# Cross attention in fp32r on one core: the stationary operands moved to other remainders by 512 bytes

## What is computed

```python
x_q = jnp.einsum('oc,bcn->bno', w_qk, y)
x_k = jnp.einsum('oc,bcn->bon', w_qk, x)
x_v = jnp.einsum('oc,bcn->bon', w_v, x) + b_v[None, :, None]
energy = jnp.einsum('bnc,bcm->bnm', x_q, x_k)
attention = jax.nn.softmax(energy, axis=-1)
attention = attention / (1e-07 + attention.sum(axis=1, keepdims=True))
x_r = jnp.einsum('bcn,bnm->bcm', x_v, attention)
x_r = jax.nn.relu(jnp.einsum('oc,bcn->bon', w_t, x - x_r) + b_t[None, :, None])
return x + x_r
```

## Time and profile before

| | us |
|---|---|
| median of 3 runs | 1866.73 |
| lowest, highest | 1864.39, 1866.74 |
| the profiled execution, its own time | 1866.61 |
| its span, first to last instruction | 1864.7 |
| TensorE matmul busy in the span | 1856.5 |
| VectorE, ScalarE, GpSimd busy | 1503.8, 1307.4, 780.7 |
| mean granted TensorE clock | 0.999 |

### The profile page before, as it was taken

One profiled execution on the slowest core, in us unless ns is written; L12 is line 12 of the kernel. 1 busy time (PEld: TensorE's weight loads), 2 busy tenths in 40 slices (PEclk: granted clock), 3 DMA queues, 4 the chain that ended last, 5 costly groups with the idle time before them and its releaser, 6 DMA issues.

```text
span 1864.7 us, 26374 instructions
## 1 busy us (share of the span) xinstructions
PE 1856.5 (100%) x8884; PEld 1565.2 (84%) x8884; DVE 1503.8 (81%) x2036; ACT 1307.4 (70%) x1793; POOL 780.7 (42%) x415
## 2 busy tenths in 40 slices
PE   9999999999999999999999999999999999999999
PEld 7888888888888888888888888888888888888887
DVE  6888787887877878878778788787787877877877
ACT  6677766677666776667766677766677666776664
POOL 4542444533444334444244452444533444424430
PEclk9999999999999999999999999999999999999999
DMA  3011211111110111101111111111011110111100
GB/s 107 30 62 46 69 67 51 39 45 68 67 68 23 64 49 67 68 23 67 45 67 68 39 51 45 67 68 62 28 52 61 68 67 23 68 45 68 68 9 37
DMA packets 33946, 101.92 MB, mean 55 GB/s; under 512 B 4208, under 2 KB 4976, under 8 KB 33904
## 3 DMA queue, kind: packets, MB, share of 16 engines
q1 hardware_dynamic: 33360, 101.46, 15.6%
q10 hardware_dynamic: 544, 0.00, 0.0%
HBM read 67.90 MB, written 33.55 MB: 54 GB/s over the span
## 4 chain that ended last, share of the span: by engine, by line
PE 97%; DVE 2%; ACT 1%; issue 0%; DVEq 0%
PE pv L693 36%; PE row_b L601 19%; PE row_a L601 14%; PE pv L669 9%; PE row_a L661 5%; PE row_b L661 5%; PE row_a L652 4%; PE row_b L652 4%; DVE colsum L445 0%; DVE p_lo L452 0%; PE pv L766 0%; DVE p_sb L427 0%; PE pv L661 0%; DVE gx_lo L387 0%; PE pv L770 0%
## 5 line engine op out<-in xcount | busy, mean ns | idle before, releaser
L201 POOL TENSOR_TENSOR y_lo<-y_raw,y_hi 128x896 fp32r<-128x896 f32 x128 | 279.1, 2203 | 566.2 <-ACT y_hi L258 377.1
L452 DVE SCALAR_TENSOR_TENSOR p_lo<-p_sb,row_inv,p_hi 128x1024 fp32r<-128x1024 f32 x256 | 328.9, 1286 | 98.3 <-ACT p_hi L304 98.3
L287 ACT ACTIVATE ev<-row_b 128x512 f32<-128x512 f32 x384 | 229.4, 597 | 202.9 <-PE row_b L601 202.9
L186 POOL TENSOR_TENSOR x_lo<-x_sb,x_hi 128x1024 fp32r<-128x1024 f32 x63 | 152.6, 2423 | 446.8 <-ACT x_hi L246 446.8
L304 ACT ACTIVATE p_hi<-p_sb,row_inv 128x1024 fp32r<-128x1024 f32 x256 | 292.4, 1142 | 32.8 <-PE pv L693 30.7
L296 ACT ACTIVATE p_sb<-p_sb,neg_max 128x1024 f32<-128x1024 f32 x256 | 295.1, 1154 | 25.5 <-DVE neg_max L427 21.5
L445 DVE SCALAR_TENSOR_TENSOR colsum<-p_sb,row_inv,colsum 128x1024 f32<-128x1024 f32 x224 | 289.6, 1293 | 8.5 <-DVE row_inv L435 0.6
L427 DVE CUSTOM_DVE_ANT_0 p_sb<-row_a,ev 128x1024 f32<-128x1024 f32 x128 | 156.5, 1223 | 146.7 <-PE row_a L601 141.8
L693 PE MATMUL pv<-p_lo,z_hi 128*128 128x512 f32 x1024 | 273.9, 389 | 0.5 <-DVE p_lo L452 0.5
L693 PE MATMUL pv<-p_hi,z_hi 128*128 128x512 f32 x1024 | 273.7, 389 | 0.0
L693 PE MATMUL pv<-p_hi,z_lo 128*128 128x512 f32 x1024 | 273.7, 389 | 0.0
(11 more groups left out here) (128 smaller groups left out, 3594.6 us busy)
## 6 DMA issues: line engine op xcount, KB each, us to landing
x_sb<-x SPq DMA_DIRECT2D x64, 512.0 KB, 4.8
out<-res SPq DMA_DIRECT2D x62, 512.0 KB, 2.9
y_raw<-y SPq DMA_DIRECT2D x64, 256.0 KB, 3.7
y_raw<-y SPq DMA_DIRECT2D x32, 512.0 KB, 3.7
out<-res SPq DMA_DIRECT2D x4, 256.0 KB, 2.0
res<-w_qk SPq DMA_DIRECT2D x1, 256.0 KB, 3.6
res<-w_t_T SPq DMA_DIRECT2D x1, 256.0 KB, 7.4
res<-w_v SPq DMA_DIRECT2D x1, 256.0 KB, 7.4
```

What stands on the lines that cost most here:

```text
L186: nc.gpsimd.tensor_tensor(x_lo[par][:, kt, :], x_sb[par][:, kt, :], x_hi[par][:, kt, :].bitcast(FP32), ALU.subtract).then_inc(x_lo_done, 1)
L201: nc.gpsimd.tensor_tensor(y_lo[:, :, cols], y_raw[:, 1:8, cols], y_hi[:, :, cols].bitcast(FP32), ALU.subtract).then_inc(y_lo_done, 1)
L287: nc.scalar.activation(ev[:, to, :], bank_b, ACT.Copy, scale=scale).then_inc(b_copied, 1)
L452: nc.vector.scalar_tensor_tensor(out=p_lo[r][:, :], in0=p_sb[r][:, :], scalar=row_inv[:, j:j + 1], in1=p_hi[r][:, :].bitcast(FP32), op0=AL ...
```

## The change

The stationary tensors g, z, wtT and y, and the moving tensor hnT, are allocated behind `res`, each pair with a gap tensor ahead that nothing reads or writes. No instruction is changed.

```diff
-        g_hi, g_lo = sb("g_hi", [P, KT, C], FP32R), sb("g_lo", [P, KT, C], FP32R)
-        hnT_hi, hnT_lo = sb("hnT_hi", [P, KT, C], FP32R), sb("hnT_lo", [P, KT, C], FP32R)
-        wtT_hi, wtT_lo = sb("wtT_hi", [P, KT, C], FP32R), sb("wtT_lo", [P, KT, C], FP32R)
...
-        y_hi, y_lo = sb("y_hi", [P, 7, BANK], FP32R), sb("y_lo", [P, 7, BANK], FP32R)
...
-        z_hi, z_lo = sb("z_hi", [P, NT, C], FP32R), sb("z_lo", [P, NT, C], FP32R)
...
         res = sb("res", [P, KT, N])
 
+
+        sb("gap_g", [P, 32])
+        g_hi, g_lo = sb("g_hi", [P, KT, C], FP32R), sb("g_lo", [P, KT, C], FP32R)
+        sb("gap_z", [P, 32])
+        z_hi, z_lo = sb("z_hi", [P, NT, C], FP32R), sb("z_lo", [P, NT, C], FP32R)
+        sb("gap_wtT", [P, 16])
+        wtT_hi, wtT_lo = sb("wtT_hi", [P, KT, C], FP32R), sb("wtT_lo", [P, KT, C], FP32R)
+        sb("gap_y", [P, 16])
+        y_hi, y_lo = sb("y_hi", [P, 7, BANK], FP32R), sb("y_lo", [P, 7, BANK], FP32R)
+        sb("gap_hnT", [P, 16])
+        hnT_hi, hnT_lo = sb("hnT_hi", [P, KT, C], FP32R), sb("hnT_lo", [P, KT, C], FP32R)
```

## The result

| | before | after |
|---|---|---|
| median, us | 1865.56 | 1889.80 |
| lowest, highest | 1864.05, 1866.74 | 1888.33, 1890.00 |
| profiled execution, its own time | 1866.61 | 1890.00 |
| its span | 1864.7 | 1888.1 |

The ratio is 1.0125, with a 95% interval of 1.0113 to 1.0137: the change makes the kernel slower, by 24 us. I had forecast no change.

What follows compares the result with a forecast made beforehand. TensorE was taken to bound the kernel, by matmul count times start spacing. Five family terms and the gaps, 0 each, left the forecast at 1866.6 us, beside a median of 1866.73; the range was 1815 to 1912.

Steps and rivals of the forecast that it cites:

- What bounds the kernel: TensorE, busy 1856.5 of 1864.7 us: time is the number of matmuls times the distance between their starts.
- The value I take: 0: Start-to-start spacing of the matmuls on TensorE: the new addresses change it by 0 ns; no change had chance 0.42.
- five families: Matmuls p on z, gx on y, x on wtT, x on g, hnT on x: spacing change forecast as 0 each.
- three rows: Trace evidence for 0: a matmul without weight load, equal 226.7 ns in L693 and L652, L661 unmoved by other SBUF users.
- The lone matmul: Matmul starting at 33.02 us, no weight load beside it: lasts 0.39 us like its neighbours, so loads cost it nothing.
- The second and third rows: L693 and L652 share no tensor or address yet have 226.7 ns; L661 keeps 119.6 ns while DMA, VectorE, GpSimd work.
- Rival A: Shifted addresses act like the late load, 5.0 ns per 512-column matmul: +36 us, 1903, or 1910 with L661; chance 0.30.
- late weight load: Load at 601.18 us, some 15 ns late: the next six distances are 231.7 ns each, 5.0 ns above the steady 226.7.
- Rival D: The chip counts distances in another unit than 512 bytes; result as in the forecast, no chance of its own.
- B: The 13 ns are a collision at distance 0: 97 us if all goes, about 1774; largest family alone 1832; chance 0.20.
- C: L661 (hnT on x) alone gets faster, 6 ns for each of 1488 matmuls, 9 us: 1858; chance 0.08.
- the 13 ns: What each fp32r matmul's spacing exceeds its columns at 2.4 GHz: 226.7 against 213.3 ns, 119.6 against 106.7.

Runs made afterwards that it cites:

- exchange of own and next distance: Matmuls alone, computation left out: both operands alternate between remainders 0 and 128, own distance 0 and next 128, then exchanged; 228.5 and 230.0 ns.
- finer map: Matmuls alone, computation left out: every distance from 0 to 252 bytes in steps of 4, 36 matmuls each; 512 columns never below 226.7 ns.

## Why the prediction was wrong

**What bounds the kernel** was right: the time is the number of matmuls times the spacing of their starts, and the whole result, 24 us, is in that spacing, while waits, clock and the other engines stood still.

**The step that failed is "The value I take: 0".** It priced the change of the spacing at nothing in each of the five families, and the runs show +5.4, +6.2 and +5.8 ns in three of them, +1.3 in p on z and -2.3 in hnT on x. Each of its three rows was read rightly, and none carried the conclusion. The lone matmul lasts as long as its neighbours, so I took it that an fp32r matmul has its excess without a load beside it, and that the address of the weights can't matter. The page of the profile says that the ends of matmuls are modelled, so a duration is a weak witness. And in the changed kernel the same matmul, again with no load beside it, lasts 397 ns instead of 388, and the second one of this kind 392 instead of 388:

```profile
32.36 0.40 PE L607 MATMUL row_a<-gx_hi,y_lo 128*128 128x512 f32 x1
34.02 0.19 PEld L607 LDWEIGHTS row_b<-gx_hi,y_hi 128*128 128x128 f32 x1 [1.70 <-ACT ev L293]
```

So in these records a matmul without a load beside it carries the cost of the new distance too, and could not tell the two cases apart. The spacing turned out to be a steady state into which a run of matmuls settles: 226.7 at one distance and 233.3 at another, and at four of twelve distances one or the other by what ran before. A single matmul at the end of a run at distance 0 tells nothing about the state at another distance. The second and third rows, that tensors and other users of SBUF don't matter, only showed that absolute addresses and the other engines don't. Every product of the kernel before stood at distance 0, so its trace held one point of the map and no slope.

**The rule of the Trainium skill** that I set beside it (page "TensorE: Matmul & The Clock Gate", section "Part 2: What happens when you issue a matmul"), that loading the next weights takes nothing from the running matmul, would have given 0 for all five families. For fp32r this 0 is wrong: the same matmuls stand at 226.7 or at 233.3 ns by the distance to their weights. Whether it is the loading that holds them up, which the rule denies, no run shows. For bf16 and plain fp32 the 0 holds, 216 ns at each distance tried. The same page's formula (section "Back-to-back issue gap") gives 215.8 ns for 512 columns and 109.2 for 256; bf16 has just these, 215.8 and 109.2, and no fp32r run reached them. The plain fp32 records that I had set beside the 215.8 have 256 columns, for which the formula gives 109.2, so they agree with it only if each is counted as 512.

**Rival A was the one that happened, without its largest family.** Its price of 5.0 ns from the late weight load was near the +5.4, +6.2 and +5.8 ns of the three families that lost, but in part by luck: the load of the earlier trace rows was 15 ns late, and with hnT alone shifted a load 46 ns late costs nothing. It was applied to all 7272 matmuls of 512 columns, and 3072 of them, p on z, moved by 256 bytes, which is a whole period. They lost 1.3 ns, behind their neighbours. This is why the result is 1890 and not 1903. Its own objection, that the spacing heals within six matmuls, was the right observation: it heals to the steady state of the distance, and the change had moved that.

**Rival D** had been given no chance, as its outcome seemed to be that of the forecast. But the pattern does repeat by another unit, 256 bytes instead of 512, and for p on z this decided about 20 us (3072 matmuls at 6.6 ns).

**Rivals B and C.** With 512 columns the 13 ns are no collision that other distances remove: over 64 distances none fell below 226.7. With 256 columns half of them can go, from 120.0 to 113.3 ns at distance 112. C was right in its sign, hnT on x gained 2.3 ns rather than 6; the 6 ns were there to be had, at distance 112, where it gained 5.8.

**The numbers.** 1889.8 lies inside the range of 1815 to 1912, and slower by over 0.2% had a chance of 0.30 while no change had 0.42. With one distance in the trace and a late load showing that a shift of one stream can cost, A deserved more than the forecast.

What stays open is the cause below the map. The exchange of own and next distance gave 228.5 and 230.0 ns, so neither of them alone sets the spacing, and a shorter weight load made it cheaper at distance 128 and dearer at 0. Which reads hold each other up, and why the spacing moves in steps, no run shows.

## What to carry to other kernels

Where fp32r matmuls of 512 columns stand back to back, the distance by 256 bytes between moving and stationary operand is worth up to 13 ns for each: keep 512-column products at distance 0 by giving all large tensors sizes of a multiple of 256 bytes and putting the small ones behind them, and look for 256-column products in a map of their own, entered from the matmuls that stand ahead of them. Gaps of 64 and 128 bytes between the operands cost 1.25% here, with no wait and no idle time to show it: compare the lengths of the chain's pieces with their counts. And a trace in which a quantity never varies can't price a change of it; where a map costs one short run, measure before arguing.

## What the runs showed of the hardware

- The spacing of fp32r matmuls of 512 columns is 226.7 ns at best, 233.3 at most distances that are multiples of 32 bytes, and 240.0 at 20, 132, 196 and 244. With 256 columns it lies between 113.3 and 123.3 (129.7 at one distance). The best distance for one need not be good for the other: 112 has 113.3 for 256 columns and 231 for 512, and 0 has 226.7 for 512 and 120.0 for 256. But 28, 60, 236 and 252 are low for both, 226.7 and 115.5 to 116.7.
- Many of the settled values stand at steps of 6.67 ns over the time of the columns at 2.4 GHz (213.3 and 106.7 ns): 33 of the 64 distances are at 226.7, 233.3 or 240.0 with 512 columns and 26 at 113.3 or 120.0 with 256, the others mostly lie between. With 320 columns it was 146.7 at all four distances tried, that is 133.3 + 13.4; with 384 it was 173.3 at 0 and 64, 176.0 at 128 and 174.7 at 192.
- A settled spacing is often the mean of a short cycle: in the finer map at 128 bytes the single distances are 229 and 237 ns in turn.
- A steady spacing is no function of the distance alone: at 240 bytes it was 226.7 or 236.8 by what ran before.
- bf16 (512 columns at five distances, 256 at three) and plain fp32 (at three) showed none of this: 215.8 and 109.2 ns for bf16, 215.8 for each record of plain fp32.
